# Causal attention in a twelve-stage kernel: the planner that deals out row maxima gets other costs for its steps

## The reference, cut to what matters

```python
att = jnp.einsum('bhid,bhjd->bhij', q, k) + bias[None]
att = att * (1.0 / math.sqrt(D))
att = jnp.where(causal[None, None], att, -jnp.inf)
att = jax.nn.softmax(att, axis=-1)
y = jnp.einsum('bhij,bhjd->bhid', att, v)
```

## Time and profile before

| | us |
|---|---|
| median of 3 runs | 3386.45 |
| lowest, highest | 3386.17, 3389.59 |
| the profiled execution, its own time | 3386.32 |
| span of its trace | 3384.5 |
| causal attention, from 2593 to 3140 | 547 |
| steps 4 to 159 of it, 2656.70 to 3117.40 | 460.7 |

### The profile page before, as it was taken

One profiled execution on the slowest core, in us unless ns is written; L12 is line 12 of the kernel. 1 busy time (PEld: TensorE's weight loads), 2 busy tenths in 40 slices (PEclk: granted clock), 3 DMA queues, 4 the chain that ended last, 5 costly groups with the idle time before them and its releaser, 6 DMA issues. The chain is left out here.

```text
span 3384.5 us, 61888 instructions
## 1 busy us (share of the span) xinstructions
PE 3007.2 (89%) x24429; PEld 1635.3 (48%) x24469; DVE 2441.6 (72%) x5485; ACT 1803.6 (53%) x3298; POOL 851.1 (25%) x809
## 2 busy tenths in 40 slices
PE   4878579898799999998899879798998899998999
PEld 3435456566323333333566557476776222333677
DVE  8898678777599999994877853735336888884433
ACT  2223347777478777776777743133222466777211
POOL 0334147766100000001966710101303111212000
PEclk8899889999799999999999989898999689899899
DMA  1065221111320000000211110001102300000100
GB/s 54 9 156 141 68 63 33 37 31 25 119 112 1 2 1 1 2 1 26 65 25 37 29 34 1 2 28 63 44 1 69 112 32 1 35 2 1 48 1 13
DMA packets 77879, 129.20 MB, mean 38 GB/s; under 512 B 12772, under 2 KB 52616, under 8 KB 77384
## 3 DMA queue, kind: packets, MB, share of 16 engines
q1 hardware_dynamic: 77592, 125.25, 13.0%
HBM read 77.39 MB, written 34.19 MB: 33 GB/s over the span
## 5 line engine op out<-in xcount | busy, mean ns | idle before, releaser
L2065 ACT ACTIVATE AR<-ps 128x1024 f32<-128x1024 f32 (+2 forms) x756 | 717.9, 996 | 247.6 <-PE ps L1966 182.1
L2152 DVE TENSOR_REDUCE AR<-ps 128x1 f32<-128x512 f32 x1296 | 809.1, 683 | 38.3 <-PE ps L1935 37.4
L1966 PE MATMUL ps<-AR 32*128 32x512 bf16 (+3 forms) x4992 | 524.2, 379 | 5.4 <-ACT AR L2065 3.8
L1935 PE MATMUL ps<-AR 32*128 32x512 bf16 (+3 forms) x1664 | 484.3, 399 | 40.2 <-DVE AR L2152 14.1
L1983 PE MATMUL ps<-AR 128*32 128x512 f32 (+3 forms) x3328 | 438.2, 600 | 9.2 <-ACT AR L2070 6.7
L2562 PEld LDWEIGHTS ps<-AR 128*128 128x128 f32 x3072 | 363.2, 192 | 60.3 <-issue 47.4
L2721 DVE SCALAR_TENSOR_TENSOR X<-ps,AR,X 128x128 f32<-128x128 f32 x512 | 143.7, 344 | 342.9 <-PE ps L2562 342.5
L1935 PEld LDWEIGHTS ps<-AR 32*128 32x128 bf16 x1664 | 121.0, 93 | 524.9 <-DVE AR L2152 392.9
L2562 PE MATMUL ps<-AR 128*128 128x128 f32 x3072 | 363.3, 276 | 0.0
L2537 PE MATMUL ps<-XT,AR 128*128 128x512 f32 x672 | 307.8, 594 | 0.1
L206 POOL TENSOR_TENSOR rs<-rs,halves 128x4 f32<-128x4 f32 x48 | 49.5, 1031 | 831.6 <-DVE rs L198 831.6
(11 more groups left out here) (326 smaller groups left out, 5010.1 us busy)
## 6 DMA issues: line engine op xcount, KB each, us to landing
AR<-AR SPq DMA_DIRECT2D x124, 128.0 KB, 2.3
band<-AR SPq DMA_DIRECT2D x32, 450.0 KB, 5.1
AR<-band SPq DMA_DIRECT2D x32, 448.0 KB, 5.2
AR<-in_c_rot SPq DMA_DIRECT2D x64, 128.0 KB, 2.3
AR<-in_L3f_w SPq DMA_DIRECT2D x30, 256.0 KB, 6.0
rows_KA<-AR SPq DMA_DIRECT2D x32, 128.0 KB, 2.4
AR<-scr_bias SPq DMA_DIRECT2D x32, 128.0 KB, 3.2
AR<-in_L2f_w SPq DMA_DIRECT2D x30, 128.0 KB, 2.7
```

Source lines behind the costliest of these rows:

```text
L1935: e.matmul(g.bank[b][:, 0:w], QA[rows, q, 128 * i:128 * i + 128], KA[rows, q, 512 * first:512 * first + w], start=way != "kept", stop=True ...
L1966: t = e.matmul(g.bank[self.base[i, u] + h % 2][:, lo:512], K[32 * h:32 * h + 32, q, 128 * kt:128 * kt + 128], Q[32 * h:32 * h + 32, q, que ...
L2065: e.activation(dst[:, :, lo:512], src[:, :, lo:512], ACT.Exp, scale=self.scale).then_inc(*s.up("exp" if u else "left", k, i, *((1,) if u e ...
L2152: e.tensor_reduce(o, g.bank[b][:, 0:w], AXX, ALU.max).then_inc(*s.up("reduced", k, n, h, st, kc))
```

## The change

The costs of the steps are replaced in the causal stage. The old cost was 0.15 plus 0.85 times the share of the 512 queries that is computed, plus 0.35 if the step has a bias. The new one is 1.0 for a step without bias, 0.67 for one with 256 biased columns and 0.46 for one with 128.

```diff
+    def free_time(self, n, kt):
+
+        near = self.near_cols(n, kt)
+        return 1.0 if not near else 0.67 if near[1] - near[0] == 256 else 0.46
+
     def hold(self, b, *closers):
 
...
         area = [(512 - self.low(n, kt)) / 512.0 for n, kt in steps]
         if causal:
-            area = [0.15 + 0.85 * x + (0.35 if self.near_cols(n, kt) else 0.0) for (n, kt), x in zip(steps, area)]
+            area = [self.free_time(n, kt) for n, kt in steps]
         self.begin, at = {}, 0.0
```

## The result

The changed kernel takes 3409.46 us (median of 4 runs, 3407.64 to 3410.48); the kernel before, timed beside it, 3388.02 us. The ratio is 1.0062, with a 95% interval of 1.0045 to 1.0079: slower by some 21 us. The forecast was 3381 us with a range to 3396.

What follows compares the result with a forecast made beforehand. TensorE and VectorE were taken as within reach of each other for some 406 us of causal attention, the later one depending on a step's maxima. 3386.4 - 2 (full clock) - 3 (clock) = 3381 us, range 3365 to 3396.

Steps and rivals of the forecast that it cites:

- The deal: Causal attention, steps 4 to 159: how many of the 624 maxima each step gets; the number differs in 68 of 156.
- The prices at full clock: Mean time per kind of step, such as plain with eight maxima 3.69 us; the full-clock sum was about -2 us.
- the classes: Steps from 4 on grouped as plain, before the diagonal, 256 biased of 512, narrower biased, last of a round, by maxima.
- half width term: Plain steps of eight maxima become wider, from 5.5 to 6.6 widths of 512: +5 us taken, bounds 0 and 10.
- The clock term: TensorE's half clock in causal attention: -9 us if five low stretches go, +6 for two or three new, net -3.
- the five old falls: Clock drops after stretches with eight maxima on VectorE and TensorE partly idle; low stretches of 30.7 us together, -9 if gone.
- The signs: Expected: 512-column diagonal steps 2.1 to 2.8 us, smaller bias wait, steps 40 to 51 about 39 us, mean clock 0.92.
- The slower rival: The burst at steps 40 to 51 decides: +3 us at full clock, +6 of clock, 3395 us; chance 0.22.
- The cost 0.46 for the step before the diagonal: This step has full score matmuls beside only 128 biased columns; seven of its 12 get no maxima, -12.3 us.
- Nothing else is late: Negated maxima close at least two steps ahead of their round's first score; group loads stay in place on the DMA queue.
- The third score pair: In causal attention, claimed to come at step 139 in place of 138.
- The rule of the Trainium skill: Cycling PSUM banks with many small TensorE idle times makes the clock go back and forth; against packing twelve maxima.

Runs made afterwards that it cites:

- e11_083: Changed kernel with 0.83 in place of 0.46 as cost of the step before the diagonal; 3391.20 us, ratio 1.0000 to the kernel before.
- e8_full_array: Changed kernel with one whole-array matmul ahead of every second maximum in steps of over four maxima; 3403.59 us, ratio 1.0040 to the kernel before.
- e12_new_full_40: Changed kernel with whole-array matmuls ahead of every second maximum of the steps of over four, in steps 40 to 51 alone; 3400.34 us, ratio 1.0035.

## Why the prediction was wrong, point by point

- **The deal.** Right: all counts came out as worked out, and the place, steps 40 to 51, was named.
- **The prices at full clock.** Right, as far as the classes show. With each kernel's own means of full-clock steps, and estimates for the four steps whose class has none, steps 4 to 159 sum to 435.9 us before and 430.5 after, -5.4 where I had about -2. The seven plain eights at full clock took 28.10 us, 4.01 each, for the 3.69 and the half width term of the forecast; the one step of twelve at full clock took 5.73, for 5.8; before the diagonal with none 12.82 over 6 is 2.14, for 2.06. The views:

```profile
sum 28.10, PE 24.16 PEld 6.65 DVE 27.07 ACT 22.04 POOL 0.64; mean PE 3.45 PEld 0.95 DVE 3.87 ACT 3.15 POOL 0.09
...
sum 12.82, PE 12.82 PEld 3.87 DVE 9.63 ACT 7.68 POOL 0.06; mean PE 2.14 PEld 0.65 DVE 1.60 ACT 1.28 POOL 0.01
...
2821.88:2827.61 5.73, 4.53 (x32) 1.42 (x31) 5.36 (x23) 2.77 (x4) 0.52 (x2) 1.00 0.00 0
```

- **The clock term: the step that failed.** I put "Two or three new falls of 6.8 us are +6. Net -3." By this the time at half clock was to shrink, by 30.7 us for the five old falls against some 14 to 20 for new ones. It grew by 51 us, from 82 to 133. At the 0.27 to 0.37 us of the pairs above that is +14 to +19, where the forecast had -3. So the price of 0.3 held, and the amount was wrong. The number of low stretches hardly changed, 13 for 12, though five were to go and two or three to come, and the new ones are long. The five of the earlier trace rows last 3.4 to 10.2 us each. With eights about, one lasted 34 us, from before step 12 through step 17, and one 20 us, through steps 40 to 43, the row below. The error in kind was to take the length of a fall from the diagonal, and to look for falls at the catch-up alone.

```profile
2793.99:2812.62 18.63, 18.32 (x106) 4.94 (x105) 14.25 (x39) 8.17 (x10) 0.00 (x0) 0.50 0.38 142
```

- **What that leaves.** Above the full-clock sums the kernel before has 24.8 us and the changed one 50.3, 25.5 more. The 7 to 12 us that the clock's price doesn't cover are a remainder, and no run shows what they are. The twelves of steps 4 and 5, all at half clock, took 8.56 and 7.36 us; what they add to it is open.
- **The signs.** ScalarE's wait for the bias fell as named, step 136 took 4.3 us for 4.5, and no diagonal step came near 5. Steps 40 to 51 took 54.0 us for about 39, and 46.2 with the clock at 1.00, with VectorE busy for 41.5; steps 52 to 67 took 49.6 for about 42; the mean clock was 0.86 for 0.92. Two signs of being wrong came: a clock of 0.68 in the burst, below 0.88, and diagonal steps without maxima over 2.8 us at full clock (36 and 100, 2.9 and 3.4).
- **The slower rival** named the right mechanism and place: the burst and the falling clock. Its price was too low, +9 for +20, and it said nothing of steps 4 to 23, which lost 8 us. The sign of the result was on its side, at a chance of 0.24.
- **The cost 0.46 for the step before the diagonal.** I named it, and counted it only through the classes. With 0.83 in its place the catch-up is no burst any more, and 18 us come back, as e11_083 shows.
- **Nothing else is late.** Right: no new wait of a load or a closed round shows. The third score pair begins at steps 139 and 140 in the two plans, not at 138 and 139; the difference of one step is as I had it.

The rule of the Trainium skill (TensorE: Matmul & The Clock Gate, A second HAM failure mode: psum-queue depth-cycling), weighed in the prediction, fits the falls: the clock goes back and forth in a stage where TensorE waits briefly and often for a bank (308 times in the changed kernel, 177 us in all). That the cycling is the cause is not shown, since no run changed the banks. The long idle gaps of that page's other advice aren't there: the longest wait on a maximum was 2.5 us, and in steps 4 to 159 of the changed kernel TensorE was never idle for more than 1.35 us.

What stays open: the split of the 8 us in steps 4 to 23 between the two twelves there and the clock (the low stretch in which step 4 begins ends at 2671 us before and at 2688 in the changed kernel), and the exact share of the clock in the 21 us of steps 40 to 51. It is at least 5.7 to 7.8 by e8_full_array, and 8 to 11 by the price above for some 31 us more at half clock. The rest goes with the maxima that moved here from other steps (76 for 52), of which steps 52 to 67 gave 3.4 back.

## What to carry to other kernels

A plan that moves work between engines' free times should be priced at both levels of TensorE's clock: ask how much time the new order spends at the low one, not only what a low microsecond costs. A planner's costs are a time axis as well as weights; when they are changed, compare the rate, the lead and the catch-up first, and scale the new costs to the old total. Look at the longest stretch above the average in the new deal, not at its class counts alone.

## What the runs showed of the hardware that I had not expected

The clock stayed at 0.50 while the records had TensorE busy for 29.18 of 29.49 us. Matmuls on 32 of the array's rows did little to raise it (0.68 to 0.73 in steps 40 to 51 with 52 more of them), while 26 on the whole array took it to 1.00 in e8_full_array and to 0.87 in e12_new_full_40. So busy time in the records did not tell whether the clock would rise.

The same list of instructions doesn't always have the same clock, as the four pairs above show. A microsecond at half clock cost 0.27 to 0.37 us there. Differences of 4 to 5 us in one stretch are as large as most gains of the later experiments, and they are why a gain in one profiled stretch was not counted without the timed runs.
